# Target-row gathers of a graph kernel: 121 rows by GpSimd's indirect transfers, 4 rows by single transfers of SyncE

## What is computed

```python
h = jnp.maximum(_layernorm(x, axis=-1), 0.0)
x = x + _L0_gnn_ref(h, edge_attr_2, ..., edge_index)   # spline convolution: messages from h[src], mean over equal dst, plus h @ root_w.T + root_b
h = jnp.maximum(_layernorm(x, axis=-1), 0.0)
x = x + _L1_gnn_ref(h, edge_index, ...)                # attention over edges and self loops, feed-forward, two layer norms
return x
```

## Time and profile before

| | |
|---|---|
| time, median of 3 runs | 3216.57 us (3211.85 to 3221.68) |
| the profiled execution | 3218.86 us, its span 3217.0 us, mean granted TensorE clock 0.801 |
| POOL / PE / DVE / ACT busy | 2469.2 / 2189.9 / 1863.1 / 850.2 us |
| transfers by POOL's queue | 64000 packets, 30.57 MB |
| transfers by SP's queue | 52070 packets, 91.52 MB |

### The profile page before, as it was taken

One profiled execution on the slowest core, in us unless ns is written; L12 is line 12 of the kernel. 1 busy time (PEld: TensorE's weight loads), 2 busy tenths in 40 slices (PEclk: granted clock), 3 DMA queues, 4 the chain that ended last, 5 costly groups with the idle time before them and its releaser, 6 DMA issues.

```text
span 3217.0 us, 33333 instructions
## 1 busy us (share of the span) xinstructions
PE 2189.9 (68%) x10666; PEld 1516.7 (47%) x10666; DVE 1863.1 (58%) x3228; ACT 850.2 (26%) x1614; POOL 2469.2 (77%) x2011
## 2 busy tenths in 40 slices
PE   2787778748877887766767158775867646588740
PEld 1555555525665665545555146553535424254430
DVE  4788989884444444333434024355687666999720
ACT  1323223213333333322323023332212221022210
POOL 8777777787878887787778778888887686248877
PEclk9889989878899888877877568776988766898775
DMA  2333333221222122112111111111111111011100
GB/s 59 83 71 76 76 75 74 49 69 31 41 40 49 34 42 44 39 36 39 32 30 30 20 15 34 34 36 35 18 27 15 23 25 26 3 23 30 36 10 10
DMA packets 116215, 123.95 MB, mean 39 GB/s; under 512 B 70726, under 2 KB 72747, under 8 KB 116070
## 3 DMA queue, kind: packets, MB, share of 16 engines
q0 software_dynamic: 64000, 30.57, 10.1%
q1 hardware_dynamic: 52070, 91.52, 9.0%
HBM read 59.51 MB, written 64.00 MB: 38 GB/s over the span
## 4 chain that ended last, share of the span: by engine, by line
POOL 56%; issue 16%; DVE 14%; PE 12%; ACT 1%; DMA 1%; POOLq 0%; DVEq 0%; ACTq 0%
POOL ring L459 33%; POOL x_table L481 15%; POOL out_rows L507 8%; DVE region L1594 3%; PE V L794 2%; PE V L563 2%; PE C L575 2%; DVE region L1586 2%; PE C L539 1%; DVE region L1293 1%; DVE region L1365 1%; PE T L524 1%; DVE region L1576 1%; PE C L569 1%; PE C L571 1%
## 5 line engine op out<-in xcount | busy, mean ns | idle before, releaser
L459 POOL DMA_INDIRECT ring<-in_x,index x800 | 983.6, 1230 | 244.4 <-issue 244.4
L507 POOL DMA_INDIRECT out_rows<-region,scatter_to x400 | 499.4, 1248 | 252.4 <-DVE region L1434 127.3
L1262 DVE TENSOR_REDUCE var<-sq 125x16 f32<-125x512 f32 x325 | 221.1, 682 | 728.1 <-ACT sq L961 727.4
L459 POOL DMA_INDIRECT ring<-x_table,index x400 | 501.5, 1254 | 124.5 <-issue 124.2
L481 POOL DMA_INDIRECT x_table<-region,index_out x400 | 481.7, 1204 | 122.9 <-issue 121.5
L563 PE MATMUL V<-xT,w_q 128*128 128x500 f32 x600 | 387.4, 785 | 68.5 <-ACT hid L972 38.9
L961 ACT ACTIVATE sq<-C 125x512 f32<-125x512 f32 x300 | 178.8, 596 | 834.4 <-PE C L575 511.9
L539 PE MATMUL C<-center,xT 128*125 128x128 f32 x1400 | 232.5, 319 | 97.2 <-ACT xT L953 61.1
L539 PEld LDWEIGHTS C<-center,xT 128*125 128x125 f32 x1400 | 211.1, 225 | 158.2 <-issue 100.3
L575 PEld LDWEIGHTS C<-w_c,hid 128*125 128x125 f32 x2400 | 282.0, 197 | 0.0
L575 PE MATMUL C<-w_c,hid 128*125 128x32 f32 x2400 | 281.7, 277 | 0.0
(11 more groups left out here) (249 smaller groups left out, 3252.4 us busy)
## 6 DMA issues: line engine op xcount, KB each, us to landing
ring<-in_x,index POOLq DMA_INDIRECT x800, 3.2
nodes<-in_x SPq DMA_DIRECT2D x25, 500.0 KB
x_table<-nodes SPq DMA_DIRECT2D x25, 500.0 KB
x_plain<-nodes SPq DMA_DIRECT2D x25, 500.0 KB
nodes<-x_plain SPq DMA_DIRECT2D x50, 250.0 KB
out_rows<-nodes SPq DMA_DIRECT2D x50, 250.0 KB
x_table<-region,index_out POOLq DMA_INDIRECT x400, 2.6
ring<-x_table,index POOLq DMA_INDIRECT x400, 2.7
```

The costliest lines, as they stand in the source:

```text
L459: pool.indirect_dma_start(out=ring[0:P, j, s * F:(s + 1) * F], out_offset=None, in_=table, in_offset=bass.IndirectOffsetOnAxis(ap=index[0: ...
L507: pool.indirect_dma_start(out=out[:, :], out_offset=bass.IndirectOffsetOnAxis(ap=scatter_to[0:P, e:e + 1], axis=0), in_=diff[0:P, e * F:(e ...
L1262: v.tensor_reduce(unit(var, k), slots(squares(k)), AX.X, ALU.add).then_inc(var_ready, 1)
```

## The change

In blocks 1 to 4 of phase B, `gather_dst` gathers 121 rows (PT = 121) in each of its 16 transfers. The rows of partitions 121 to 124 are fetched by SP: for each of the four partitions it loads the 16 row numbers of the chunk from `index` into registers (one TENSOR_LOAD) and issues 16 transfers of one row, each with its address from a register. They stand in SP's turn "e2" of the block before, two partitions behind the store of x1 and two behind the store of base. Ahead of them SP waits for `index_in[j]` and `ring_used`, as POOL does. TensorE's "e1" waits for these rows too (`few_in[j]`). Block 0 and the gathers of phases A and D are as before, and so are all scatters.

```diff
+PT = 121
@@ sync
+            def few_rows(j, rows):
+                for p in rows:
+                    _, of = nc.values_load_multi_w_load_instructions(index[p:p + 1, j, :], engines=[mybir.EngineType.SP], min_val=0, max_val=N - 1,
+                                                                       skip_runtime_bounds_check_because="the transfer checks its own address")
+                    for s in range(CE):
+                        sp.dma_start(ring[p:p + 1, j, s * F:(s + 1) * F], x[bass.ds(of[s], 1), :]).then_inc(few_in[j], 16)
...
                 if "e2" in at:
                     j = at["e2"][0]
                     sp.wait_ge(x1_ready, b * NJ + j + 1)
                     sp.dma_start(x1_dst[bass.ds(b * NJ + j, 1), :, :].rearrange("a p w -> (a p) w"), unit(rows_out, j)).then_inc(x1_saved[j], 16)
+                    if more:
+                        sp.wait_ge(index_in[j], 16 * NB + 16 * (b + 2))
+                        sp.sem_inc(few_begun, 1)
+                        sp.wait_ge(ring_used, NC + (b + 1) * NJ + j + 1)
+                        sp.sem_inc(few_begun, 1)
+                        few_rows(j, range(PT, PT + 2))
                 if "e4" in at:
...
+                if "e2" in at and more:
+                    few_rows(at["e2"][0], range(PT + 2, P))
@@ gpsimd
-            def gather(table, j):
+            def gather(table, j, rows=P):
...
-                        out=ring[0:P, j, s * F:(s + 1) * F], out_offset=None, in_=table,
-                        in_offset=bass.IndirectOffsetOnAxis(ap=index[0:P, j, s:s + 1], axis=0)).then_inc(ring_dma[j], 16)
+                        out=ring[0:rows, j, s * F:(s + 1) * F], out_offset=None, in_=table,
+                        in_offset=bass.IndirectOffsetOnAxis(ap=index[0:rows, j, s:s + 1], axis=0)).then_inc(ring_dma[j], 16)
...
-                    gather_dst(b + 1, j)
+                    gather_dst(b + 1, j, PT)
@@ tensor
                     pe.wait_ge(ring_dma[j], (NB + b + 1) * DMAS)
+                    if not isinstance(b, int) or b > 0:
+                        pe.wait_ge(few_in[j], b * (P - PT) * DMAS)
                     t["e1"] = transpose(unit(ring, j))
```

More of the change, by code:

```diff
@@ L259, in gnn_program @@
         x1_saved = [sem(f"x1_saved{j}") for j in range(NJ)]
+        few_in = [sem(f"few_in{j}") for j in range(NJ)]; few_begun = sem("few_begun")
         rows_landed = [sem(f"rows_landed{j}") for j in range(NJ)]
@@ L470, in _, with gather_dst @@
             gather_phase(x[:, :], 0, 0)
-            def gather_dst(b, j):
+            def gather_dst(b, j, rows):
                 pool.wait_ge(index_in[j], 16 * NB + 16 * (b + 1))
                 pool.wait_ge(ring_used, NC + b * NJ + j + 1)
-                gather(x[:, :], j)
+                gather(x[:, :], j, rows)
             def scatter_x1(c, j):
@@ L486, in _ @@
             for j in range(NJ):
-                gather_dst(0, j)
+                gather_dst(0, j, P)
             for j in range(NJ):
```

## The result

The changed kernel takes **3491 us** (median) against 3216 for the one before, a ratio of 1.085 (95% interval 1.082 to 1.088): 275 us slower, where 86 us faster was forecast. The profiled execution took 3494.3 us around a span of 3492.5. One of the four executions was in a slower state (3897 us at a granted clock of 0.543, against 0.774 in the profiled one) and the ratio leaves it out.

A forecast was written before the change was run, and what follows sets the result against it. POOL's transfers were taken as the bound. 320 gathers, each 0.27 us shorter, save 86 us and SyncE's added work costs nothing, so 3216.6 - 86 = 3130 us, with a range of 3062 to 3235.

The forecast's parts named there:

- What bounds the kernel: From first x1 scatter to next phase's first gather, POOL's transfers bound; shorter gathers shorten it one for one, up to about 150 us.
- a shift is carried to the end: The next phase begins with POOL's gathers and everything waits for these, so the gain reaches the span's end.
- Part 1, the gathers: 320 gathers in blocks 1 to 4 have 11 entries a queue, not 25: 0.27 us less each, 86 us in all.
- Rivals C and D: C: cost follows rows, 11 us gained, 3205, chance 0.06; D: gathers cost the same whatever they hold, 3217, chance 0.06.
- Part 2, SyncE: SyncE's added row transfers and register loads bring it to 38 us a chunk (33 to 47), under POOL's 44.8: no cost.
- 64 x 0.40 = 25.7: SyncE's 64 one-row transfers a chunk at 0.40 us each take 25.7 us.
- the rest: SyncE's existing work a chunk: 7.3 us for units' stores and loads, about 1.2 for x1's store, base's store and index load.
- r: SyncE's us a chunk in the loop: it decides from 45.7 on, and from 50 the whole gain is gone.
- rival E: SyncE's row transfers or register loads too slow: decides from 50 us a chunk, each us beyond adds 20 us; chance 0.13.
- Do the added transfers slow POOL?: Whether SyncE's transfers lengthen POOL's: taken as nothing, against a possible 3.4 us a chunk, 68 in all.
- 38.1 us a chunk: Pace at which the other engines make x1 ready, ahead of POOL's 49.1, as long as nothing holds TensorE up.
- until 81.1 + 68.6 are used up: TensorE's 81.1 us pause before the next gathers and 68.6 us of gather waits: cover for about 150 us of gain.

The follow-up runs named there:

- POOL's part alone: Kernel before with 121-row gathers in blocks 1 to 4, SyncE's row transfers and register loads left out: 3351.4 us on chip 10.
- the runs of chip 7: Kernel before 3216.2 us; with 121-row gathers and two SyncE waits, no row transfers, 3352.9; whole change with its semaphores declared last 3502.1.

## Why the forecast was wrong, step by step

- **What bounds the kernel**, and that a shift is carried to the end: right. On chip 12, 320 gathers of 0.188 us less gave 57 us, and in the changed kernel the part after the stretch is 1384 us against 1378.
- **Part 1, the gathers**: right in kind. The trace has 3520 packets of 1408 B (11 rows), 320 x 11, and 1600 of 44 B (11 entries of 4 B), 320 x 5, for the queues without rows. The size was 0.18 to 0.21 us rather than 0.27, well within the stated 0.10 to 0.45. The Trainium skill's remark that descriptor generation is a small cost that shows only late (DMA: Bandwidth & Descriptors, anatomy of a GpSimd DMA, cited in the forecast) doesn't fit: some 12 to 18 ns an entry show from the first entries on. Rivals C and D fall as well: 110 rows cost what 121 do, and 124 cost more than 125.
- **Part 2, SyncE**: this step failed, at the term "64 x 0.40 = 25.7". Its 0.40 us were built from a static transfer and register operations in rows without any stall, and that price is right where these don't stall: 0.42 us with POOL idle or silent, and 0.35 for fixed addresses even beside POOL. But in the changed kernel a transfer with its address from a register takes 0.81 us beside POOL's work. The mean of all is 0.68, thus 44 us a chunk where 25.7 were taken; the 80 register loads took 151 us, 7.6 a chunk where 4 were taken (median 1.3 us, mean 1.9). With the 8.5 us that the forecast has for the rest, r is 60, beyond the 50 at which rival E decides, and x1 indeed came every 60 us from chunk 4 to chunk 19. That rival had the place right (the store of base behind the rows, ScalarE waiting for it 105.8 us). Its formula gives (60 - 50) x 20 = 200 us over 3217, and SyncE's part measured 149 on chip 7, but over 3353, where x1 was late already; that the two are near is partly luck. E had 0.13, and with it went the only warning.
- **Do the added transfers slow POOL?** Right: 1063 ns a gather beside SyncE's transfers, 1054 without them.
- **The step that wasn't there.** The forecast took it that the other engines keep their 38.1 us a chunk whatever POOL does, and used it as cover ("until 81.1 + 68.6 are used up"). They went to 53.0 with POOL's part alone on chip 10 and to 57.1 in the changed kernel (chunks 1 to 14). This term, put at nothing, is the larger one: 194 us by the runs of chip 7, where SyncE's is 149. No row of the kernel before has a "remote" wait, so its size couldn't be read; but that all POOL transfers in it had 125 rows, which the forecast said of their price, held for their side effects too.
- The chip wasn't a term either. On chip 12, POOL's part gives 3161 us, 31 above the forecast. With the 0.42 us of a transfer without such stalls, r would be 27 + 7.6 + 8.5 = 43, under POOL's chunk of 49.1 - 16 x 0.19 = 46; so by this estimate the whole change could have come near 3161 there. It wasn't tried.

## What to carry to other kernels

An instruction's price beside other engines' work is not its price alone, and it can depend on the form: take it from rows with the same form and the same company, or keep the doubled price as a rival with real weight. When a run's time lands in a theory's range, look in its trace for the mechanism too; the run with fixed addresses had the time of a theory whose mechanism its trace refutes. Pace that other engines "have in reserve" is a term of the sum, and it must be bounded when the form of the traffic changes. And when two runs of nearly the same kernel differ by more than their edits can explain, put both on one chip before forming a theory: two theories here were built on differences between chips.

## What the hardware showed unexpectedly

- One kernel took 3161 us on one chip and 3351 on another, while a second kernel took 3218 and 3215 on them.
- An indirect transfer of n rows costs POOL by n over its largest divisor up to 16: 1.02 us for 121, 1.23 for 125, 1.33 for 124, 1.67 for 122.
- A one-row transfer of SyncE with its address from a register takes 0.42 us with POOL idle and 0.81 beside POOL's transfers in the changed kernel; with a fixed address it takes 0.35 beside them. The difference is in single instructions of 0.7 us, register operations of 0.03 us among them.
- With late signals, matmuls that wait for nothing start in groups 0.7 us apart, and a signal from TensorE to ScalarE can take 12 us.
